# Back pipeline: the rows of the second and third norm made on GpSimd, the attention's gelu taken directly behind that of the MLP

## What is computed

```
h = token embeddings (three hashed n-gram tables)
h = h + phase attention(norm(h))
h = h + graph-gated experts(norm(h))       # graph attention over 262144 edges picks 2 of 4 experts
h = h + head attention(norm(h))            # the "second norm", below
h = h + top-k MLP(norm(h))                 # the "third norm", below
norm(x) = (x - mean(x)) / sqrt(var(x) + eps)
head attention(x): q, k, v = x @ W_qkv + b; k, v normed per head of 4 channels;
    kv = k^T v / 256, per sequence and head; proj = (q @ kv + x) @ W_proj + b; gelu(proj) + x
top-k MLP(x): route = x @ wr; the best 127 rows of each sequence get
    (gelu_tanh(x @ w1 + b1) @ w2 + b2) * route; every row gets + x
```

## Time and profile before

| | us |
|---|---|
| median of 3 runs | 5116.01 (5111.89 to 5119.61) |
| the profiled execution's own time | 5124.35 |
| its span | 5122.5 |
| busy in the span: TensorE | 3072.0 (60%) |
| VectorE | 2808.3 (55%) |
| ScalarE | 2358.2 (46%) |
| GpSimd | 2231.7 (44%) |
| steps 4 to 27 of the back pipeline | 4677.77 to 4999.19 |

### The profile page before, as it was taken

The page is one execution under the profiler, slowest core; times in us unless marked ns, Lnnn a source line. Parts: engine busy times, 40 slices in busy tenths (PEclk is TensorE's granted clock), DMA queues, the critical chain, the costliest instruction groups (busy, mean ns, idle before and its releaser), DMA issues. The chain is left out here.

```text
span 5122.5 us, 63233 instructions
## 1 busy us (share of the span) xinstructions
PE 3072.0 (60%) x21149; PEld 2328.3 (45%) x21149; DVE 2808.3 (55%) x5784; ACT 2358.2 (46%) x4288; POOL 2231.7 (44%) x2218
## 2 busy tenths in 40 slices
PE   3646663665565665665665665665665665625775
PEld 2435552554454454454454544544544544523443
DVE  8857882454454454454454454454544544558885
ACT  3635665444344344344344444444444443405775
POOL 7866613334434334344344344344344344435520
PEclk8667675777777777777777777777777777766776
DMA  2111101111111111111111111111111111112101
GB/s 58 24 22 21 21 6 44 24 23 34 24 26 27 28 27 31 24 27 31 23 27 31 23 27 31 23 27 31 23 27 30 23 32 26 21 44 55 54 2 33
DMA packets 157528, 145.13 MB, mean 28 GB/s; under 512 B 71240, under 2 KB 133080, under 8 KB 156776
## 3 DMA queue, kind: packets, MB, share of 16 engines
q1 hardware_dynamic: 88656, 109.49, 6.4%
q0 software_dynamic: 68768, 34.45, 6.1%
HBM read 92.97 MB, written 50.82 MB: 28 GB/s over the span
## 5 line engine op out<-in xcount | busy, mean ns | idle before, releaser
L937 PE MATMUL es_pgot<-hash_space,es_pick 128*128 128x256 bf16 x13056 | 1836.0, 288 | 1424.2 <-issue 1403.9
L857 POOL DMA_INDIRECT es_got<-node_table,late x1632 | 1551.7, 951 | 2124.4 <-DVEq L1077 1646.9
L937 PEld LDWEIGHTS es_pgot<-hash_space,es_pick 128*128 128x128 bf16 x13056 | 1299.8, 101 | 1903.6 <-issue 1747.5
L1019 DVE TENSOR_TENSOR es_prod<-es_pgot,es_own 128x512 f32<-128x512 f32 x272 | 187.8, 690 | 1800.7 <-PE es_pgot L937 1620.5
L871 ACT ACTIVATE es_pick<-es_away,consts 128x512 bf16<-128x512 f32 x1088 | 680.0, 711 | 7.0 <-DMA es_away<-sorted_keys 6.7
L293 POOL DMA_INDIRECT fr_ring<-in_emb,fr_rows x384 | 459.6, 1197 | 203.5 <-issue 112.5
L875 ACT ACTIVATE es_pick<-es_pick,consts 128x4096 bf16<-128x4096 bf16 x136 | 503.6, 3703 | 0.9
L894 ACT ACTIVATE ex_hid<-ex_phid,weights 128x256 f32<-128x256 f32 x128 | 53.8, 471 | 707.6 <-PE ex_phid L944 707.3
L1039 DVE TENSOR_TENSOR es_hot<-es_iota,late 128x1024 bf16<-128x1024 f32 x272 | 331.6, 1219 | 35.4 <-DVE es_st L1079 25.7
L1040 DVE TENSOR_TENSOR es_hot<-es_iota,late 128x1024 bf16<-128x1024 f32 x272 | 330.1, 1214 | 0.0
L910 ACT ACTIVATE ex_y<-ex_py 128x512 f32<-128x512 f32 x64 | 38.2, 597 | 574.6 <-remote 553.3
(11 more groups left out here) (351 smaller groups left out, 4334.8 us busy)
## 6 DMA issues: line engine op xcount, KB each, us to landing
es_away<-sorted_keys SPq DMA_DIRECT2D x68, 512.0 KB
es_got<-node_table,late POOLq DMA_INDIRECT x1632
edge_states<-es_st SPq DMA_DIRECT2D x68, 384.0 KB
expert_outputs<-ex_y SPq DMA_DIRECT2D x64, 256.0 KB
bk_y<-expert_outputs SPq DMA_DIRECT2D x8, 2048.0 KB
fr_ring<-in_emb,fr_rows POOLq DMA_INDIRECT x384
out_dram<-h SPq DMA_DIRECT2D x4, 1024.0 KB, 5.1
late<-in_edges SPq DMA_DIRECT2D x1, 2048.0 KB, 9.0
```

Of the source, the lines that this page charges most:

```text
L857: pool.indirect_dma_start(out=got[:, r, k, :], out_offset=None, in_=table_dram, in_offset=bass.IndirectOffsetOnAxis(ap=src[:, n, k:k + 1]. ...
L937: mm = pe.matmul(p_got[:, q, c * 256:c * 256 + 256], pick[:, r, q // 2, k, at * P:at * P + P], parts[:, part, k], start=(k == 0 and part = ...
```

## The change

Three things change, all in `back`:

- GpSimd makes `x2` and `x3`. VectorE keeps the reciprocals and signals them (`rstd2`, once in 16 tiles, behind the centring of q = 3; `rstd3`, once a step). GpSimd makes `x3` of slot `mlp` as its first work of a step, and `x2` of slot `new + 1` as its last.
- On VectorE the reciprocal of `rstd3` stands at the head of the step, ahead of part 0, where it was behind the passes over k and v.
- ScalarE's gelu of the attention stands directly behind the gelu of the MLP (and the squares of q = 2), ahead of `x3t` and the squares of k and v.

```diff
--- before.py
+++ after.py
@@ -1306,7 +1306,7 @@
             sem(n) for n in ("xt", "sq", "qt", "std", "gj", "std3", "x3t", "hid", "yt"))
         (s_xt_p, s_kv_p, s_q_p, s_kvm_p, s_o_p, s_prj_p, s_x3_p, s_hid_p, s_yt_p, s_y_p, s_rw_p) = (
             sem(n) for n in ("xtp", "kvp", "qp", "kvmp", "op", "prjp", "x3p", "hidp", "ytp", "yp", "rwp"))
-        s_hx2, s_kv, s_hx3, s_sd = (sem(n) for n in ("hx2", "kv", "hx3", "sd"))
+        s_hx2, s_kv, s_hx3, s_sd, s_rstd2, s_rstd3 = (sem(n) for n in ("hx2", "kv", "hx3", "sd", "rstd2", "rstd3"))
         s_var_g, s_std_g, s_less, s_exp, s_read, s_xc2, s_sq2, s_sum2, s_std2, s_used = (
             sem(n) for n in ("varg", "stdg", "less", "exp", "read", "xc2", "sq2", "sum2", "std2", "used"))
         s_w, s_w_p, s_kept, s_kept_p, s_done, s_out = (sem(n) for n in ("w", "wp", "kept", "keptp", "done", "out"))
@@ -1353,10 +1353,25 @@
                 if g < GN:
                     gather(g, [q * ST + t for t in these])
 
+            def second_rows(s):
+
+                pool.wait_ge(s_rstd2, s // GS + 1)
+                if s >= 2:
+                    pool.wait_ge(s_hx2, s - 1)
+                    pool.wait_ge(s_xt_p, s - 1)
+                nc.gpsimd.tensor_tensor(x2[:, s % 2], by_half(xc[:, slot(s)]), by_half(spread(rstd2[:, slot(s)], D)), ALU.mult).then_inc(s_x2, 1)
+
             for n in range(-10, 0):
                 gathers(n, range(ST))
+            second_rows(0)
             for n in range(STEPS):
                 new, normed, mlp = n, n - 1, n - 3
+                if is_slot(mlp):
+                    pool.wait_ge(s_rstd3, mlp + 1)
+                    if mlp >= 2:
+                        pool.wait_ge(s_hx3, mlp - 1)
+                        pool.wait_ge(s_x3_p, mlp - 1)
+                    nc.gpsimd.tensor_tensor(x3[:, mlp % 2], by_half(xc[:, slot(mlp)]), by_half(spread(rstd3[:, slot(mlp)], D)), ALU.mult).then_inc(s_x3, 1)
                 gathers(n, range(2))
                 if is_slot(new):
                     pool.wait_ge(s_x2, new + 1)
@@ -1365,6 +1380,8 @@
                 if is_slot(mlp):
                     pool.wait_ge(s_x3, mlp + 1)
                     nc.gpsimd.tensor_tensor(by_half(h[:, slot(mlp)]), by_half(h[:, slot(mlp)]), x3[:, mlp % 2], ALU.add).then_inc(s_hx3, 1)
+                if is_slot(new + 1):
+                    second_rows(new + 1)
 
         @block.scalar
         def _(act):
@@ -1427,6 +1444,11 @@
                         a.activation(hid[:, m].rearrange("p (b t) -> p b t", b=SB), p_hid[:, :, m * T:m * T + T], ACT.Gelu_apprx_tanh, bias=W("m_b1")[:, m:m + 1]).then_inc(s_hid, 1)
                 if q == 2 and g + 1 < GN:
                     gate_squares(g + 1)
+                if is_slot(joined):
+                    act.wait_ge(s_prj_p, joined + 1)
+                    if joined >= 2:
+                        act.wait_ge(s_xc3, joined - 1)
+                    a.activation(gj[:, joined % 2].rearrange("p two b d -> p (two b d)"), p_prj, ACT.Gelu).then_inc(s_gj, 1)
                 if is_slot(mlp):
                     act.wait_ge(s_x3_p, mlp + 1)
                     a.activation(x3t[:], p_x3, ACT.Copy).then_inc(s_x3t, 1)
@@ -1435,11 +1457,6 @@
                     if new >= 1:
                         act.wait_ge(s_var, new)
                     a.activation(sq_kv[:], groups(new), ACT.Square).then_inc(s_sq, 1)
-                if is_slot(joined):
-                    act.wait_ge(s_prj_p, joined + 1)
-                    if joined >= 2:
-                        act.wait_ge(s_xc3, joined - 1)
-                    a.activation(gj[:, joined % 2].rearrange("p two b d -> p (two b d)"), p_prj, ACT.Gelu).then_inc(s_gj, 1)
                 if is_slot(last):
                     act.wait_ge(s_yt_p, last + 1)
                     if last >= 1:
@@ -1564,6 +1581,11 @@
                 dve.wait_ge(s_sq2, g + 1)
                 v.tensor_reduce(rstd2[:, tiles(g)], sq_h[:], AX.X, ALU.add).then_inc(s_sum2, 1)
 
+            def root_back(g):
+
+                dve.wait_ge(s_std2, g + 1)
+                v.reciprocal(rstd2[:, tiles(g)], rstd2[:, tiles(g)]).then_inc(s_rstd2, 1)
+
             ch.step(v.memset(ones[:], 1.0))
             for name in ("kv_w", "kv_b"):
                 by_head = W(name).rearrange("p (g c) -> p g c", c=C1)
@@ -1616,17 +1638,13 @@
                     gate_rows(0)
                     norm_centre(0)
                     norm_sums(0)
+            root_back(0)
             for n in range(STEPS):
                 new, normed, joined, mlp = n, n - 1, n - 2, n - 3
                 g, q = n // GS, n % GS
-                if is_slot(new):
-                    if q == 0:
-                        dve.wait_ge(s_std2, g + 1)
-                        do(v.reciprocal(rstd2[:, tiles(g)], rstd2[:, tiles(g)]))
-                    if new >= 2:
-                        dve.wait_ge(s_hx2, new - 1)
-                        dve.wait_ge(s_xt_p, new - 1)
-                    v.tensor_tensor(x2[:, new % 2], by_half(xc[:, slot(new)]), by_half(spread(rstd2[:, slot(new)], D)), ALU.mult).then_inc(s_x2, 1)
+                if is_slot(mlp):
+                    dve.wait_ge(s_std3, mlp + 1)
+                    v.reciprocal(rstd3[:, slot(mlp)], rstd3[:, slot(mlp)]).then_inc(s_rstd3, 1)
                 gates_at(q, 0, g)
                 if is_slot(normed):
                     dve.wait_ge(s_std, normed + 1)
@@ -1635,13 +1653,6 @@
                     dve.wait_ge(s_norm, normed + 1)
                     do(v.tensor_tensor(halves(normed), halves(normed), repeat(W("kv_ln_w"), 2), ALU.mult))
                     v.tensor_tensor(halves(normed), halves(normed), repeat(W("kv_ln_b"), 2), ALU.add).then_inc(s_kv, 1)
-                if is_slot(mlp):
-                    dve.wait_ge(s_std3, mlp + 1)
-                    do(v.reciprocal(rstd3[:, slot(mlp)], rstd3[:, slot(mlp)]))
-                    if mlp >= 2:
-                        dve.wait_ge(s_hx3, mlp - 1)
-                        dve.wait_ge(s_x3_p, mlp - 1)
-                    v.tensor_tensor(x3[:, mlp % 2], by_half(xc[:, slot(mlp)]), by_half(spread(rstd3[:, slot(mlp)], D)), ALU.mult).then_inc(s_x3, 1)
                 gates_at(q, 1, g)
                 if is_slot(normed):
                     dve.wait_ge(s_kvm_p, normed + 1)
@@ -1657,6 +1668,8 @@
                     do(v.tensor_tensor(by_half(h[:, slot(joined)]), by_half(h[:, slot(joined)]), gj[:, joined % 2], ALU.add))
                     do(v.tensor_reduce(mean3[:, slot(joined)], h[:, slot(joined)], AX.X, ALU.add))
                     v.scalar_tensor_tensor(out=xc[:, slot(joined)], in0=spread(mean3[:, slot(joined)], D), scalar=-1.0 / D, in1=h[:, slot(joined)], op0=ALU.mult, op1=ALU.add).then_inc(s_xc3, 1)
+                if q == 3 and g + 1 < GN:
+                    root_back(g + 1)
                 gates_at(q, 2, g)
             dve.wait_ge(s_rw_p, 1)
             do(v.tensor_scalar(rw[:].rearrange("p (s b two) -> p s two b", two=2, b=SB), p_rw, W("route_b"), None, ALU.add))
```

## The result

The changed kernel takes 5143.45 us (median of 5 runs, 5139.61 to 5153.80), the kernel before 5111.89 (5 runs). The ratio is 1.0054, with a 95% interval of 1.0036 to 1.0071: slower, by 31.6 us in the medians. Forecast were +31 us, 5147.

What follows compares the result with a forecast made beforehand. No engine was taken as the bound: a step is a loop of waits across VectorE, TensorE and ScalarE. Turns 22.6, collisions 6 and start 2.4 gave +31 us on 5116, 5147; the forecast case's ends were 5130 to 5172.

Steps and rivals of the forecast that it cites:

- The serial turn: Steps 4 to 27: part 0 queues behind the wait for `rstd3`, turns become serial; 344.0 us against 321.4, plus 22.6.
- q = 3: Steps at this place: the exp's table load stands on the way of `qt` and hides the clock; turn 14.2 us.
- The gelu: ScalarE: gelu and table load hidden ahead of `x3t`, margin 0.4 us; passes to `qt` 5.55 us instead of 5.9.
- The rows on GpSimd: `x3` and `x2` themselves hidden; collisions with VectorE's passes over k and v cost 6 us, ends 0 and 20.
- the rule taken to its end: GpSimd contending with both two-input passes over k and v in every step: 26 us instead of 6.
- The start: `x2` of slot 1 comes late, behind GpSimd's first gathers and sum: 2.4 us, between 0 and 5.
- The sum: Whole kernel: 22.6 for the turns, 6 for collisions, 2.4 for the first steps, together +31 us.
- The range's far end: Slow end of the forecast case: 22.6 + 13.5 + 20 = +56 us, giving 5172.
- (1): Faster: part 0 stays covered, `rstd3` arrives before VectorE gets there; about 5102 us; chance 15%.
- (2): No change: TensorE at its higher clock behind the passes gives back 22 us, collisions cost nothing; 5116 to 5126; 12%.
- (3): GpSimd becomes the bound: its round of 16 us at q = 0 and 1 passes the turn; +20 on top, 5167; 13%.

Runs made afterwards that it cites:

- e2: Kernel before with only the reciprocal of `rstd3` and its wait moved ahead of part 0: +36.4 us, ratio 1.0100 to the kernel before.
- e3: Changed kernel with the reciprocal of `rstd3` put behind part 0, directly ahead of that of `sd`: +4.0 us, ratio 1.0010 to the kernel before.
- e6: Changed kernel with only the attention's gelu back behind the squares of k and v: +44.1 us, ratio 1.0078 to the kernel before.
- e4: Kernel before with `x2` and `x3` on GpSimd, reciprocal of `rstd3` behind part 0, gelu in its old place: +11.6 us, ratio 1.0029.
- e8: Kernel before with the gelu forward, only `x3` on GpSimd and the reciprocal of `rstd3` behind part 0: -3.2 us, ratio 0.9989.
- e1_gelu_alone: Kernel before with only the attention's gelu moved forward, ahead of `x3t`: -12.0 us, ratio 0.9957 to the kernel before.
- e9_gelu_total_later: Kernel before with the gelu forward and the gate pieces of q = 1 one place later: -12.9 us, ratio 0.9979.
- e12: Kernel before with only the attention's gelu moved forward, run again on another chip: -18.3 us, ratio 0.9967 to the kernel before.
- e7: Kernel before with the gelu forward and only `x2` on GpSimd: -15.5 us, ratio 0.9978 to the kernel before.

## Why the prediction was right

**The serial turn.** The step of the prediction that carried it was that part 0 now queues behind the wait for `rstd3`. The trace shows it as described, e2 shows it alone (+36.4), e3 shows it undone. The reciprocal of `sd` was put at 3.5, 4.4, 4.3 and 3.0 us behind the load, and came at 3.6, 4.4, 4.4 and 2.8 on average (the last includes step 27 without part 0; in step 24 GpSimd's operations fall on the softmax weights and it is 4.3). The turns were put at 13.9, 14.8 and 14.7 and came at 14.36, 14.73 and 14.51. Steps 4 to 27 were put at 344 us and took 347.6, or 348.9 from load to load, collisions included.

**q = 3** was mis-sized: 14.2 us forecast, and 15.3 measured for the five steps with a part 0. In four of the five GpSimd's sum of `x2` falls on the passes, which take 4.0 us instead of 3.13, and `qt` comes 6.8 us behind them on average, not 6.35. The longer passes, 3.5 us in all, belong to the collisions that the prediction counts apart. Some 2 us are left, and step 27 went the other way, 10.7 instead of 12.6, with a `qt` only 3.57 us behind the passes. These two nearly cancel, by luck.

**The gelu.** Forecast was 5.55 us from the passes to `qt` at q = 0 to 2; measured 5.43. Hidden with a margin, as said. In steps 5 to 31 TensorE's matmuls no longer wait for `yt`; its weight loads do, 3.0 us in 9 steps, where it was 19.3 in 26. Before the change the shortest of these 18 times was 5.1 us (step 16), not the 5.7 that the prediction starts from.

**The rows on GpSimd.** 6 us were put down for collisions. The passes are 9.2 us longer in all: 1.8 in steps 2 and 3, 6.1 in steps 4 to 27 and 1.2 in 28 to 31. All executions of the second and third pass in the changed kernel:

```profile
L1654 DVE TENSOR_TENSOR bk_kv<-bk_kv,weights x32: 691/742/1175, 4634.0 to 5070.6; 128x512 f32<-128x512 f32 x32
...
L1655 DVE TENSOR_TENSOR bk_kv<-bk_kv,weights x32: 691/692/1098, 4634.7 to 5071.3; 128x512 f32<-128x512 f32 x32
```

The Trainium skill, "GPSIMD Engine Reference", Key points, names instructions with two SBUF inputs among those that contend. The trace agrees for the second and third pass, up to 1.18 and 1.10 us, while the first, which reads PSUM, kept 0.69 beside a sum (step 25). Two collisions in every step, as the rule taken to its end would have it (26 us), didn't come: at q = 1 and 2 the sums mostly fall elsewhere.

Why the rows cost no more here is only in part shown. With `rstd3` ahead of part 0 no product `y` is long (at most 2.34 us, in e6 too); in e3, e4 and e8, where no wait stands ahead of part 0, it goes up to 3.09. But the wait alone doesn't make the rows cheap: e4 has the long products and costs 8.4 us of back part, less than the 10.6 that the rows cost behind the wait (e6 against e2). The 17 to 19 us come where the gelu is forward and the wait stands behind part 0 (e3, e8); there the prediction's list of what can collide, the passes, is too short. The kernel with the gelu and `rstd3` moved and the rows on VectorE was not run, so what the rows cost in the changed kernel isn't measured by itself. GpSimd's product took 0.61 us alone, less than the 0.73 of the sum taken for it.

**The start** is the term whose mechanism the runs don't bear out. It was put at 2.4 us for the late `x2` of slot 1; 3.9 were lost up to step 4. The second `x2`, now GpSimd's, did start later, 8.5 us behind the first in place of 7.4. But the reciprocals of `sd` of steps 1 and 2 stand 10.1 and 19.7 us behind the first `x2`, and before the change 10.2 and 19.5, so the late `x2` cost 0.2 us at most. The loss comes behind them: passes of 4.00 us instead of 3.13 in steps 2 and 3, beside a GpSimd sum, and a reciprocal 3.45 us behind the load in step 4 instead of 2.19, the wait for `rstd3` again. e2, with nothing new on GpSimd, loses 2.0 us up to step 4. That a term of about this size stood in the sum was luck.

**The sum.** 31 forecast, 30.4 measured in the back part, is closer than its terms. In steps 4 to 27 the turns grew by 26.1 us with 7 us of collisions in them (6.1 on the passes, 0.9 on the softmax weights of step 24), so the serial turns with the gelu cost some 19, an estimate, instead of 22.6; the collisions were more than was put down, and the start was made of both. The range's far end, +56, also leaves out the start, which was itself given up to 5 us.

**The rivals.** (1), faster, was to decide where VectorE reaches the head of a step later than 1.8 us behind the load. It was idle there for 2.9, 2.0, 2.5 and 1.6 us on average (q = 0 to 3). (2) needed TensorE at its higher clock behind the passes. From step 4 on that came in step 27 alone, where the mean granted clock is 1.00; in all others `qt` came 4.9 us or more behind the passes. (3) needed a GpSimd round above the turn; ScalarE waited for the transposes of `x2` once, for 1.2 us.

## What to carry to other kernels

An instruction that waits takes everything behind it on its engine along: before moving one forward by a few lines, ask what is now queued behind the wait and whether it used to fill that wait. Moving a table load into a wait that another engine sets was free here, and a gain. Work that goes to GpSimd takes its own times with it: a sum released by VectorE starts behind VectorE's next operation, a sum released by GpSimd's own queue may start in front of it, and then VectorE pays. And where two moves are made at once, run each alone: the gelu's gain hid part of what the order cost.

## What the runs showed of the hardware

In steps 28 to 30, where no gate work is left, TensorE's clock level made more difference than the edits did. TensorE in step 29 of e1_gelu_alone in order of time, and its granted clock over the three steps (window, us, busy, granted clock, DMA share, GB/s):

```profile
3301.56 0.71 PE L1716 MATMUL bk_pkvm<-bk_kv 128*128 128x128 f32 x4 [1.77 <-DVE bk_kv L1637]
3302.10 0.44 PE L1723 MATMUL bk_px<-consts,bk_x 128*128 128x128 f32 x2
3302.47 1.08 PE L1734 MATMUL bk_phid<-bk_hid,weights 128*64 128x256 f32 x8
```

```profile
3285.77:3317.24 31.47, 24.02 (x146) 1.00 0.00 1
```

And the changed kernel's step 29 and its same three steps:

```profile
5033.88 1.22 PE L1729 MATMUL bk_pkvm<-bk_kv 128*128 128x128 f32 x4 [2.14 <-DVE bk_kv L1655]
5034.89 0.64 PE L1736 MATMUL bk_px<-consts,bk_x 128*128 128x128 f32 x2
5035.45 1.98 PE L1747 MATMUL bk_phid<-bk_hid,weights 128*64 128x256 f32 x8
```

```profile
5015.96:5054.82 38.86, 30.23 (x146) 0.78 0.00 1
```

In the first the clock stands at 2.4 GHz (1.00) throughout, and the second MLP product takes 1.08 us. In the second it had fallen to 1.2 GHz before `kvm`, behind an idle time of 2.14 us instead of 1.77, and the same product takes 1.98. `qt` comes 5.88 us behind the passes instead of 3.54, and the three steps take 38.9 us instead of 31.5. The passes end 0.38 us later in the changed kernel, through collisions. That this is what makes the clock fall isn't shown, and the clock falls without it too. e9_gelu_total_later does the same work as e1 in these steps, with passes of 3.13 us; its step 29, TensorE's `kvm` and the granted clock over the step:

```profile
5013.01 1.22 PE L1720 MATMUL bk_pkvm<-bk_kv 128*128 128x128 f32 x4 [1.77 <-DVE bk_kv L1641]
```

```profile
5009.82:5022.86 13.04, 10.70 (x48) 0.74 0.00 1
```

The idle time of 1.77 us is that of e1, the clock has fallen all the same, and the step takes 13.04 us instead of 10.50. Steps 28 to 31 take 43.2 us in e1, 44.9 in its repeat e12, 47.5 in e9 and 47.7 in e7, with the passes at 3.13 us in all four. What decides the level is open, and differences of some 4 us between single profiles can come from it alone.

Some 1630 of the 1720 us between the chips lie in the edge stream: its matmuls of L937 run from 844.6 to 4530.9 us in the kernel before and from 778.1 to 2830.9 in e1_gelu_alone. The waits there (waiting instruction <- what it waited for: us in total, times, longest), first in the kernel before, then in e1_gelu_alone on the chip where the program takes 1720 us less:

```profile
DVE es_prod L1019 <- PE es_pgot L937: 1584.4, 81, 25.7
...
PE es_pgot L937 <- issue: 1334.3, 1136, 3.1
```

```profile
DVE es_prod L1019 <- PE es_pgot L937: 48.7, 41, 3.8
```

In the first TensorE waits 1334 us for nothing that the profile shows, between matmuls of one line, and VectorE waits for it. In the second that wait of TensorE's is not in the list, and the granted clock is 0.95 there instead of 0.75. What makes one chip so is open. The back pipeline takes the same on both: e1_gelu_alone, on the one, and e12_gelu_alone_again, on the other, differ by 2.9 us in it, and the changed kernel's two by 1.6.
